# Value product of an attention kernel with rounded part and remainder side by side: six matmuls a pair instead of nine, the blocks summed by three engines

## The reference

```python
q = (xn @ w_q).reshape(B, SQ, NUM_HEADS, DIM_HEAD)
kv = context @ w_kv
k, v = jnp.split(kv, 2, axis=-1)
scores = jnp.einsum('bqhd,bkhd->bhqk', q * SCALE, k)
attn = jax.nn.softmax(scores, axis=-1)
out = jnp.einsum('bhqk,bkhd->bqhd', attn, v).reshape(B, SQ, INNER)
out = out @ w_out + b_out
```

## Time and profile before

| | |
|---|---|
| median of 3 runs | 1105.08 us (1101.88 to 1107.95) |
| the profiled execution | 1108.28 us, of which 1106.5 us span |
| TensorE busy | 1037.5 us, 94% |
| VectorE busy | 804.1 us, 73% |
| ScalarE busy | 715.5 us, 65% |
| GpSimd busy | 522.5 us, 47% |
| value product (L2003), 1152 matmuls | 203.4 us put down to it |

### The profile page before, as it was taken

How to read it: one execution, slowest core, us unless ns; L and a number is a source line. 1 busy time by engine, 2 the same in 40 slices (tenths; PEclk the granted TensorE clock), 3 DMA queues, 4 the chain that set the end, 5 groups by cost and what they waited for, 6 DMA issues and landing times. The chain is left out here.

```text
span 1106.5 us, 22422 instructions
## 1 busy us (share of the span) xinstructions
PE 1037.5 (94%) x7055; PEld 958.6 (87%) x7055; DVE 804.1 (73%) x2017; ACT 715.5 (65%) x1853; POOL 522.5 (47%) x748
## 2 busy tenths in 40 slices
PE   4899999999999999999999999999998778889995
PEld 4899899999998999999999999999997658889983
DVE  4646787868687877778786868787776865866665
ACT  4645767676767767676767676766766545646650
POOL 5413245464554546454545454454644324564450
PEclk9989999999999999999999999999999989989998
DMA  6332122222322232322222222222123612354479
GB/s 180 99 95 73 43 51 71 58 69 55 85 60 78 56 86 54 78 70 51 63 55 71 55 72 53 64 61 67 47 50 81 198 54 84 123 162 161 135 208 287
DMA packets 79362, 98.47 MB, mean 89 GB/s; under 512 B 14460, under 2 KB 71422, under 8 KB 79249
## 3 DMA queue, kind: packets, MB, share of 16 engines
q1 hardware_dynamic: 69856, 79.04, 27.1%
q0 software_dynamic: 8848, 16.96, 4.5%
q10 hardware_dynamic: 544, 1.05, 0.3%
HBM read 41.98 MB, written 23.03 MB: 59 GB/s over the span
## 5 line engine op out<-in xcount | busy, mean ns | idle before, releaser
L940 POOL TENSOR_TENSOR prob<-prob,rinv 112x750 f32<-112x750 f32 x128 | 184.2, 1439 | 247.0 <-DVE rinv L1614 246.7
L1032 ACT ACTIVATE prob<-ps_s,negmax 112x375 f32<-112x375 f32 x256 | 144.2, 571 | 60.0 <-DVE negmax L1608 57.2
L1621 DVE TENSOR_TENSOR pT_lo<-ps_pt,pT_hi 125x672 fp32r<-125x672 f32 x128 | 108.5, 847 | 64.2 <-ACT pT_hi L1169 64.2
L1712 PE MATMUL ps_kv<-ctxT_hi,wkv 128*128 128x376 f32 x512 | 138.4, 351 | 2.5 <-DVE v_lo L1281 1.4
L1608 DVE TENSOR_REDUCE negmax<-ps_s 112x2 f32<-112x750 f32 x128 | 118.8, 928 | 1.8 <-PE ps_s L1960 1.7
L1712 PE MATMUL ps_kv<-wkv,ctxT_hi 128*125 128x512 f32 x384 | 110.3, 409 | 1.1 <-DVE k_low L1277 0.2
L1022 ACT ACTIVATE v_hi<-ps_kv 125x512 fp32r<-125x512 f32 x96 | 57.4, 597 | 78.8 <-PE ps_kv L1712 78.7
L1970 PE MATMUL ps_pt<-ident,prob 112*125 112x112 f32 x768 | 104.4, 272 | 2.3 <-POOL prob L940 2.3
L899 POOL DMA_INDIRECT places<-ysb,place_i x72 | 70.7, 982 | 71.5 <-ACT ysb L1105 59.2
L1169 ACT ACTIVATE pT_hi<-ps_pt 125x672 fp32r<-125x672 f32 x128 | 93.6, 732 | 6.8 <-PE ps_pt L1970 1.1
L1970 PEld LDWEIGHTS ps_pt<-ident,prob 112*125 112x125 f32 x768 | 94.8, 190 | 2.6 <-POOL prob L940 2.5
(11 more groups left out here) (313 smaller groups left out, 2719.5 us busy)
## 6 DMA issues: line engine op xcount, KB each, us to landing
kx<-k_low SPq DMA_DIRECT2D x256, 94.0 KB, 2.2
xg<-rows_by_expert SPq DMA_DIRECT2D x72, 128.0 KB, 2.1
qx_hi<-qx_hi SPq DMA_DIRECT2D x64, 112.0 KB, 2.3
zb<-places SPq DMA_DIRECT2D x16, 448.0 KB, 15.1
ctx_in<-in_ctx SPq DMA_DIRECT2D x16, 375.0 KB
stage_w<-in_L_ffn_mlp_w SPq DMA_DIRECT2D x16, 256.0 KB, 5.4
arena<-in_L_ffn_mlp_w SPq DMA_DIRECT2D x16, 256.0 KB, 5.9
stage_w<-in_L_xattn_w_kv SPq DMA_DIRECT2D x4, 512.0 KB, 12.0
```

What stands on the lines that cost most here:

```text
L940: e_prob.done(eng.tensor_tensor(prob[0:TQ, p % 2, :, :], prob[0:TQ, p % 2, :, :], rinv[:, 2 * p:2 * p + 2].unsqueeze(2).broadcast_to([TQ, ...
L1032: e_exp.done(eng.activation(prob[0:TQ, p % 2, half, :], S[0:TQ, half, 0:SK], ACT.Exp, bias=negmax[:, h:h + 1], accum_out=rowsum[:, h:h + 1]))
L1621: e_pt_lo.done(eng.tensor_tensor(pT_lo[:, :, :, :].rearrange("p h k t -> p h (k t)"), PT[0:KEYT, :, 0:NKEY * TQ], pT_hi[:, :, :, :].bitcas ...
L1712: last = eng.matmul(out_, lhs(i, k), rhs(j, k), start=(n == 1), stop=(n == KT * len(PASSES)))
```

## The change

Values and transposed probabilities are kept with rounded part and remainder side by side: `vx` has for each head 64 columns of the one and 64 of the other, `pTx` has both for each head. One matmul for a head and a third of the keys then gives four blocks: 128 rows (rounded values, remainders) by 2 x 112 columns (rounded probabilities, remainders). Three blocks are wanted; the fourth (remainder by remainder) is made and not used. The three are summed outside: ScalarE copies block (remainder values, rounded probabilities) of both heads to `o_sum` and (rounded values, remainder probabilities) to `oT`; VectorE adds (rounded, rounded) and `o_sum` into `o_add`; GpSimd adds `o_add` to `oT`. For SBUF room, `base_row` and `xm` become one buffer, and the table `done_by` moves into `prob1T`, filled near the end by a count and a cast instead of 120 memsets.

```diff
-        v_hi = t("v_hi", [128, NKEY, INNER], F32R)
-        v_lo = t("v_lo", [128, NKEY, INNER], F32R)
+        vx = t("vx", [128, NKEY, NH, 2, DH], F32R)
-        pT_hi = t("pT_hi", [KEYT, 2, NKEY, TQ], F32R)
-        pT_lo = t("pT_lo", [KEYT, 2, NKEY, TQ], F32R)
+        pTx = t("pTx", [KEYT, 2, 2, NKEY, TQ], F32R)
+        pT_hi, pT_lo = (pTx[:, n, :, :, :] for n in range(2))
...
+        numbers = prob1T[0:TQ, :, :].rearrange("p k t -> p (k t)")
+        number_i, done_by = numbers[:, 0:12 * YB].bitcast(I32), numbers[:, 12 * YB:24 * YB]
...
-        base_row = t("base_row", [TQ, D])
-        xm = t("xm", [TQ, D])
+        base_row = xm = t("xm", [TQ, D])
...
+        o_sum = t("o_sum", [64, 2, TQ])
+        o_add = t("o_add", [128, TQ])
...
+        v_heads = vx[:, :, :, :, :].rearrange("p k h j d -> p k j h d")
+        O_ALL = OT[:, 0:4 * TQ].rearrange("p (h j t) -> p h j t", h=2, j=2)
...
     GpSimd, constants():
-                for n in range(YB):
-                    for j in range(12):
-                        eng.memset(done_by[:, n, j:j + 1], float(n + YB * j))
     GpSimd, tail, xm in slot 32:
                     if tb.off:
-                        eng.wait_ge(kv_dve, KV_LO[KV_USE["e", 0, tb.off - 1] + 1])
+                        eng.wait_ge(f_base, 16 * tb.off)
+                    else:
+                        eng.wait_ge(s_b2, 1)
     GpSimd, slot 38 of the last batch:
+                if g == AT_NUMBERS:
+                    e_n.wait_ge(eng, BATCH[B - 1], 3)
+                    eng.iota(number_i, pattern=[[1, 12 * YB]], base=0, channel_multiplier=0).then_inc(s_numbers, 1)
+                    eng.wait_ge(s_numbers, 1)
+                    eng.tensor_copy(done_by, number_i).then_inc(s_numbers, 1)
     GpSimd, every slot, behind tail(g) and ahead of the scaled probabilities:
+                for p in range(NP):
+                    st = due(g, AT_O[p] + 1)
+                    if st:
+                        e_o_sum.wait_ge(eng, st, p + 1)
+                        e_oT.done(eng.tensor_tensor(oT[:, p, :], oT[:, p, :], o_add[:, :], ALU.add))
     ScalarE, odd slots (L1156):
                             e_o.wait_ge(eng, st, p + 1)
+                            e_o_sum.wait_ge(eng, st, p)
+                            eng.activation(o_sum[:, :, :], O_ALL[64:128, :, 0, :], ACT.Copy)
                             for half in range(2):
-                                rows_ = slice(64 * half, 64 * half + 64)
-                                last = eng.activation(oT[rows_, p, :], OT[rows_, half * TQ:(half + 1) * TQ],
+                                last = eng.activation(oT[64 * half:64 * half + 64, p, :], O_ALL[0:64, half, 1, :],
                                                       ACT.Copy)
-                            e_oT.done(last)
+                            e_o_act.done(last)
     VectorE, projections, kind "e" (L1258):
-                    if step.off:
-                        eng.wait_ge(f_base, 16 * step.off)
     VectorE, behind tail(g) and ahead of pT_lo:
+                for p in range(NP):
+                    st = due(g, AT_O[p] + 1)
+                    if st:
+                        e_o_act.wait_ge(eng, st, p + 1)
+                        e_oT.wait_ge(eng, st, p)
+                        for half in range(2):
+                            last = eng.tensor_tensor(o_add[64 * half:64 * half + 64, :], O_ALL[0:64, half, 0, :],
+                                                     o_sum[:, half, :], ALU.add)
+                        e_o_sum.done(last)
     TensorE, slot 2p+4 (L2003):
                         e_pt_lo.wait_ge(eng, st, p + 1)
-                        e_oT.wait_ge(eng, st, p)
-                        n = 0
-                        for i, j in PASSES:
+                        e_o_sum.wait_ge(eng, st, p)
+                        for half in range(2):
                             for k in range(NKEY):
-                                n += 1
-                                last = eng.matmul(OT[:, 0:2 * TQ].rearrange("p (h t) -> p h t", t=TQ),
-                                                  vv[i][0:KEYT, k, p * 128:(p + 1) * 128],
-                                                  pT[j][:, :, k, :], start=(n == 1),
-                                                  stop=(n == NKEY * len(PASSES)))
+                                last = eng.matmul(O_ALL[:, half, :, :],
+                                                  vx[0:KEYT, k, 2 * p + half, :, :].rearrange("p j d -> p (j d)"),
+                                                  pTx[:, :, half, k, :], start=(k == 0), stop=(k == NKEY - 1))
                         e_o.done(last)
```

More of the change, by code:

```diff
@@ L428, in program @@
         s_fill, f_filled, f_spare, f_zero = sem("s_fill"), sem("f_filled"), sem("f_spare"), sem("f_zero")
-        s_pad, s_blank = sem("s_pad"), sem("s_blank")
+        s_pad, s_blank, s_numbers = sem("s_pad"), sem("s_blank"), sem("s_numbers")
         s_plan, f_list, f_list_p = sem("s_plan"), [sem(f"f_list{n}") for n in range(2)], sem("f_list_p")
@@ L459, in program @@
         e_o = event("e_o", NP)
+        e_o_act, e_o_sum = event("e_o_act", NP), event("e_o_sum", NP)
         e_oT = event("e_oT", NP)
@@ L486, in program @@
         qk = (qk_hi, qk_lo)
-        vv = (v_hi, v_lo)
-        pT = (pT_hi, pT_lo)
+        v_heads = vx[:, :, :, :, :].rearrange("p k h j d -> p k j h d")
+        O_ALL = OT[:, 0:4 * TQ].rearrange("p (h j t) -> p h j t", h=2, j=2)
         AT_S = [2 * p for p in range(NP)]
@@ L513, in program @@
         AT_SEND = (41, 42, 43, 44)
-        AT_BLANK = LAST_BODY + 24
+        AT_BLANK, AT_NUMBERS = LAST_BODY + 24, LAST_BODY + 38
         ZERO = BATCH[0]
@@ L1021, in projection @@
                 if kind == "v":
-                    ins = eng.activation(v_hi[0:KEYT, n % NKEY, n // NKEY * 512:(n // NKEY + 1) * 512],
-                                         bank[0:KEYT, :], ACT.Copy)
+                    heads = slice(n // NKEY * NP, (n // NKEY + 1) * NP)
+                    ins = eng.activation(v_heads[0:KEYT, n % NKEY, 0, heads, :],
+                                         bank[0:KEYT, :].rearrange("p (h d) -> p h d", d=DH), ACT.Copy)
                 ins.then_inc(kv_act, 1)
@@ L1121, in _ @@
                 if g % 2 == 0:
[L1122 to L1126, removed]
-                                rows_ = slice(64 * half, 64 * half + 64)
-                                last = eng.activation(oT[rows_, p, :], OT[rows_, half * TQ:(half + 1) * TQ],
-                                                      ACT.Copy)
-                            e_oT.done(last)
                     tail(g)
@@ L1279, in projection @@
                 if kind == "v":
-                    at = slice(n // NKEY * 512, (n // NKEY + 1) * 512)
-                    ins = eng.tensor_tensor(v_lo[0:KEYT, n % NKEY, at], bank[0:KEYT, :],
-                                            v_hi[0:KEYT, n % NKEY, at].bitcast(F32), ALU.subtract)
+                    heads = slice(n // NKEY * NP, (n // NKEY + 1) * NP)
+                    ins = eng.tensor_tensor(v_heads[0:KEYT, n % NKEY, 1, heads, :],
+                                            bank[0:KEYT, :].rearrange("p (h d) -> p h d", d=DH),
+                                            v_heads[0:KEYT, n % NKEY, 0, heads, :].bitcast(F32), ALU.subtract)
                 ins.then_inc(kv_dve, 1)
@@ L1550, in make_plan @@
                     ct.wait_ge()
-                    ct(eng.tensor_tensor(done_by[:, :, :], sums[:, 0:1].unsqueeze(2).broadcast_to([TQ, YB, 12]),
-                                         done_by[:, :, :], ALU.is_gt))
+                    eng.wait_ge(s_numbers, 2)
+                    ct(eng.tensor_tensor(done_by, sums[:, 0:1].broadcast_to([TQ, 12 * YB]), done_by, ALU.is_gt))
                     ct.wait_ge()
-                    ct(eng.tensor_reduce(span[:, 0, 0:YB], done_by[:, :, :], AX.X, ALU.add))
+                    ct(eng.tensor_reduce(span[:, 0, 0:YB], done_by.rearrange("p (j n) -> p n j", n=YB), AX.X, ALU.add))
                     ct.wait_ge()
```

1 line of the change is left out of this document (removed).

## The result

The changed kernel takes 1141.83 us (median of 4 runs, 1140.2 to 1142.12), the kernel before 1103.92 (4 runs, 1101.88 to 1107.95): 1.032 times, 95% interval 1.0286 to 1.0353. It is slower, as forecast, but by 38 us instead of 21, and outside the range.

The account below looks back on a forecast made before the run. TensorE, 99% busy in the body, was taken as the bound on average; added work in its waits makes periods 1.6 us longer: 22.4 - 2.7 + 1.0 = +20.7 on 1105.1, so 1126 us, range 1086 to 1136.

Parts of the forecast that it names:

- Step (a): VectorE's nearly full stretch, 508.7 to 526.5: three new sums push pT_lo back 1.04 us, the product behind it about +1.0.
- the sum: Whole-run total: 14 periods give 22.4 us, first batch gives back 2.7, last batch costs 1.0; +20.7 in all.
- The price of a matmul: TensorE's value products: each of the six new matmuls keeps 0.111 us, saving 0.33 per pair and 2.7 per period.
- rival 4: TensorE's six matmuls take 0.167 us each, so the count saves nothing and the stalls stand; some 1150 us, 2%.
- the sums' prices: Added work per pair: VectorE's two sums 0.60 us, ScalarE's extra copy 0.36, GpSimd's sum 0.43.
- Where it decides: The product of 526.54 begins 0.06 us after VectorE's pT_lo ends, without slack; starting no later would favour full gain.
- rival 1: Idle time on VectorE and ScalarE takes the added work, so all of 43 us is had; 1063 us, 8%.
- rivals 2 and 3: Across periods: only part of the saving is lost, 1090 us, 14%; or stalls cancel it, within 5 of 1105, 11%.
- Step (b): GpSimd's probabilities of 525.82 wait for VectorE's sum and GpSimd's own; TensorE's transposes of them begin at +1.14 us.
- Steps (c) to (e): Later in the period, longer ScalarE copies and VectorE sums delay pT_hi (+1.08 us), nT (+1.29) and the keys' remainder (+2.04).
- three hops: Last batch: ScalarE, VectorE and GpSimd in turn ahead of the output projection cost about 1.0 us.

Follow-up runs that it names:

- copy alone: Changed kernel with ScalarE's third copy kept but VectorE's and GpSimd's sums left out, output incomplete: 1113.49 us, the kernel before 1104.79 there.
- probabilities first: Changed kernel with GpSimd's own sum behind the scaled probabilities instead of ahead of them: 1137.06 us.
- row first: Changed kernel with GpSimd's row product (L861) ahead of the four small entries instead of behind them: 1141.05 us.
- sums behind the remainder: Changed kernel with VectorE's two sums behind the remainder pT_lo of their slot and GpSimd's sum behind the probabilities: 1158.55 us.

## Why the prediction was right in sign and short in size

Sign, place and waits were right; two terms were too small. Step (a) had no cost for what GpSimd's later work does to VectorE (0.26 per period), and the sum took the first batch with a tail for a regular period (2.0 short), the last batch for 1.0 (1.3 short) and the end of the program for nothing (3.9 short).

**The price of a matmul** held (0.111, rival 4 out), as did the sums' prices: 0.56 for my 0.60, 0.35 for 0.36, 0.42 for 0.43. No overlap between sums into different halves, as weighed.

**Where it decides** held: the product of pair 2 stands behind pT_lo, and rival 1's condition is not met. Rival 1 falls with it, and rivals 2 and 3 with the period, which is 2.0 us longer and not shorter or equal.

**Step (a)** was short by 0.26, and this is most of the miss of 0.37 per period. I let the first sum vanish in the idle of 0.67 ahead of x1 and had x1 0.16 early; it came 0.07 late, and pair 1, which I had at -0.16, at +0.15. The cost of VectorE's neighbour was not in the sum: GpSimd's added work moved its row product onto L1348, which then took 0.66 instead of 0.41. Removing that overlap, in either of two ways, gave back 0.22 to 0.25.

**Step (b)** was false: prob's delay is real (transposes 0.05 behind it) but something else held that step just as long, ScalarE's copy by the run with the copy alone (9.49). The number (+1.14 for +1.32) came out near by luck, since (a) and that copy had made pair 3 late already.

**Steps (c) to (e)** named the right waits. The runs show what they hide: the copy costs 1.54 per period, VectorE's sums 1.44 on top, GpSimd 0.28, and the saved matmuls give back only 1.29. 1.54 + 1.44 + 0.28 - 1.29 = 1.97. I walked 1.6, with 0.33 given back at three places; without sums and copy, too, the whole 0.33 shows at only three of the eight products (pairs 0, 4 and 7).

**Outside the periods** I was 7.9 of 13.1 us short. The first batch gave 2.0 for 2.7. The first batch with a tail lost 3.6: one step of 13.34 for 11.04, in which TensorE waits 2.42 us for the keys' copy, and the granted clock is 0.85 behind it:
```profile
118.98 0.30 PEld L1724 LDWEIGHTS ps_kv<-ctxT_hi,wkv 128*128 128x128 f32 x2 [2.42 <-ACT kx L1031]
```
```profile
110.00:120.00 10.00, 7.22 (x45) 6.47 (x46) 8.28 (x18) 4.80 (x14) 4.68 (x6) 0.98 0.14 36
120.00:130.00 10.00, 9.41 (x59) 8.45 (x58) 6.27 (x14) 7.03 (x20) 1.81 (x2) 0.85 0.18 40
```
A wait at this place is there in the kernel before too (1.68 us, step 11.04). What it costs goes with the clock behind it (the wait, the granted clock of the 10 us behind it, the step):

| kernel | wait | clock | step |
|---|---|---|---|
| before | 1.68 | 1.00 | 11.04 |
| six matmuls, no sums | 1.90 | 1.00 | 11.03 |
| copy and VectorE sums | 2.23 | 1.00 | 11.27 |
| nine matmuls with sums | 2.42 | 1.00 | 11.79 |
| probabilities first | 2.30 | 0.83 | 12.88 |
| copy alone | 2.43 | 0.83 | 13.10 |
| the changed kernel | 2.42 | 0.83 | 13.34 |
| row first | 2.43 | 0.83 | 13.34 |
| sums behind the remainder | 2.95 | 0.83 | 13.55 |

With the clock at 1.00 the step is 0.8 us longer at most, and at 0.83 it is 1.8 to 2.5 longer. So most of this loss is a few us of TensorE at its lower level, for which the prediction had no term. The last batch lost another period's worth, 2.3, where I had three hops for 1.0, and the part behind the last product 3.9, where I had nothing. The granted clock of that last part is 0.92 against 0.94 in the kernel before, and over these two and the eleven runs on the first three chips of the experiments its length goes with the clock: 224.0 to 226.7 us in the four at 0.95 to 0.97, 226.4 to 229.1 in the four at 0.94, 228.0 to 232.0 in the five at 0.91 to 0.93. Kernels with all sums are among the shortest (224.0 for nine matmuls, 226.7 with the probabilities first), so these 3.9 us are not shown to come from the change; what sets the clock there stays open.

**The range** took 2.2 per period as its upper end, which held, but gave the parts outside the periods no upper end at all. They alone carried the result past 1136. Another 2.7 us of the miss is the base: I took off 3.2 for the profiled execution of the kernel before, and the changed kernel's profiled execution stands only 0.3 above its median.

## What to carry to other kernels

Matmuls saved on a full TensorE are worth less than their time (here 1.29 of 2.7 us), since its waits for the other engines grow. An engine that is busy 36 of 50 us can still make its added work count: eight copies of 0.35 us on ScalarE, ahead of everything that feeds TensorE, cost 1.54 per period, spread over four of its eight steps. Before an accumulation in PSUM is replaced by blocks to be summed, look at who must drain the bank before the next product can begin: with one bank, each new reader stood in that path in both places tried. And a walk through one period prices the period; start and end need a range of their own.

## What the runs showed of the hardware that was not expected

- A VectorE operation with two SBUF operands took 0.66 instead of 0.41 us beside a GpSimd product in SBUF that overlapped it by 0.38.
- TensorE's granted clock fell after a wait of 1.25 us in eleven periods of one execution, and after the same wait (1.24) it did not in three later periods of that execution, nor in any regular period on another chip (0.97 against 1.00 from 500 to 550).
- A fall behind a wait of 2.42 us made one step some 1.6 us longer (13.34 with it; 11.79 in another kernel with the same wait and no fall).
- Chips differ: the kernel before took 1099.9, 1104.8, 1104.9, 1127.3 and 1135.5 us on five of them, and the mean granted clock of these executions (0.985, 0.983, 0.982, 0.985 and 0.978) does not account for it.
